# Head products of an attention kernel: from one 98-row product a head to pairs of heads on the array's row halves

## What is computed

```
n1 = ln(x); q, k, v = n1 @ wq[m] + bq, n1 @ wk[m] + bk, n1 @ wv[m] + bv
attn = softmax(q @ k.T / 4)                      # 512 x 512 for each of 2 x 16 heads
x = x + sum_m probs[m] * ((attn @ v) @ wo[m] + bo[m])
x = x + sum over the top 2 of 8 experts of gate * (gelu(ln(x) @ fw1[e]) @ fw2[e])
```

## Time and profile before

| | |
|---|---|
| median of 3 runs | 1408.23 us (1405.15 to 1408.82) |
| the profiled execution's own time | 1407.98 us |
| its span | 1406.2 us |
| mean granted clock | 0.995 |
| busy | PE 98%, DVE 76%, ACT 65%, POOL 26% |

### The profile page before, as it was taken

How to read it: one execution, slowest core, us unless ns; L and a number is a source line. 1 busy time by engine, 2 the same in 40 slices (tenths; PEclk the granted TensorE clock), 3 DMA queues, 4 the chain that set the end, 5 groups by cost and what they waited for, 6 DMA issues and landing times. The chain is left out here.

```text
span 1406.2 us, 22227 instructions
## 1 busy us (share of the span) xinstructions
PE 1380.4 (98%) x7666; PEld 714.5 (51%) x7666; DVE 1074.6 (76%) x2299; ACT 911.4 (65%) x1708; POOL 361.0 (26%) x351
## 2 busy tenths in 40 slices
PE   8999999999999999999999999999999999999989
PEld 6644445554455544456445654555445555354456
DVE  6789878977698777986879777897779868688631
ACT  3367567756667667776577666775676765657751
POOL 7422341302313223113322034132132222221000
PEclk9999999999999999999999999999999999999999
DMA  4065075321744136530662308441174415352002
GB/s 118 17 79 89 2 79 88 67 55 31 105 62 78 59 44 105 86 55 31 85 96 54 69 16 106 76 76 61 28 109 77 75 31 62 46 69 54 21 12 90
DMA packets 92307, 90.15 MB, mean 64 GB/s; under 512 B 16482, under 2 KB 87266, under 8 KB 91294
## 3 DMA queue, kind: packets, MB, share of 16 engines
q1 hardware_dynamic: 92196, 88.73, 38.1%
HBM read 35.05 MB, written 4.25 MB: 28 GB/s over the span
## 5 line engine op out<-in xcount | busy, mean ns | idle before, releaser
L1710 ACT ACTIVATE prob<-psum 128x512 f32<-128x512 f32 x1024 | 560.6, 600 | 317.9 <-PE psum L910 217.2
L1411 DVE TENSOR_REDUCE mx<-psum 128x1 f32<-128x512 f32 x1024 | 640.6, 681 | 77.8 <-PE psum L880 75.3
L895 PE MATMUL psum<-qst,kst 98*128 98x512 bf16 x1024 | 340.7, 382 | 2.3 <-DMA qst<-mrow 1.3
L880 PE MATMUL psum<-kst,qst 96*128 96x512 bf16 x1024 | 305.1, 381 | 5.5 <-DVE resid L1283 2.2
L910 PE MATMUL psum<-prob,vst 128*17 128x512 f32 x2048 | 246.6, 598 | 0.4 <-ACT prob L1710 0.2
L895 PEld LDWEIGHTS psum<-qst,kst 98*128 98x128 bf16 x1024 | 94.9, 98 | 202.8 <-issue 136.5
L880 PEld LDWEIGHTS psum<-kst,qst 96*128 96x128 bf16 x1024 | 97.5, 97 | 127.7 <-ACT prob L1710 17.1
L1861 POOL CAST parts<-resid 128x512 bf16<-128x512 f32 x64 | 39.4, 616 | 404.0 <-DVE resid L1283 404.0
L910 PEld LDWEIGHTS psum<-prob,vst 128*17 128x17 f32 x2048 | 46.7, 96 | 128.8 <-issue 109.8
L867 PE MATMUL psum<-w,cxT 128*128 128x256 f32 x448 | 105.1, 381 | 0.0
L848 PE MATMUL psum<-n2T,x 128*128 128x512 f32 x224 | 102.0, 592 | 0.0
(11 more groups left out here) (244 smaller groups left out, 1708.3 us busy)
## 6 DMA issues: line engine op xcount, KB each, us to landing
kst<-parts SPq DMA_DIRECT2D x186, 128.0 KB, 4.6
qst<-parts SPq DMA_DIRECT2D x186, 128.0 KB, 5.5
cmat<-G_dram SPq DMA_DIRECT2D x7, 1024.0 KB, 4.7
x<-in_L_ffn_fw SPq DMA_DIRECT2D x14, 512.0 KB, 3.6
w<-in_L_ffn_fw SPq DMA_DIRECT2D x14, 512.0 KB, 4.1
xbuf<-in_x SPq DMA_DIRECT2D x8, 512.0 KB, 5.2
kin<-in_ctx SPq DMA_DIRECT2D x8, 512.0 KB, 4.5
out<-acc SPq DMA_DIRECT2D x7, 512.0 KB, 3.9
```

The costliest lines, as they stand in the source:

```text
L880: e.matmul(psum[:, u.bank, :], qst[0:KROWS, h, t * P:(t + 1) * P], kst[0:KROWS, h, :], start=True, stop=True).then_inc(u.full, 1)
L895: e.matmul(psum[:, u.bank, :], kst[0:KROWS + 2, h, g * P:(g + 1) * P], qst[0:KROWS + 2, h, :], start=True, stop=True).then_inc(u.full, 1)
L1411: e.tensor_reduce(mx[:, qq * QUAD + j, t:t + 1], psum[:, u.bank, :], AX, ALU.max).then_inc(u.free, 1)
L1710: e.activation(prob[:, g % 2, j, :], psum[:, u.bank, :], ACT.Exp).then_inc(u.free, 1)
```

## The change

1. `kst` and `qst` become [128, 2, 16, 512]: partition halves for the two heads of a pair, a second index for the pass, 16 pairs. Pass 0 has the first four terms (64 rows a head); pass 1 has the last two terms, the two rows of the maximum, and zeros elsewhere.
2. A maximum is pass 0 alone: two products of 64 rows, on the row halves, into two neighbouring banks (`take_two`), and one reduction of 128 x 2 x 512. The last two terms are thus left out of the maximum, not of the score.
3. A score is two passes of two products, and one exponential of 128 x 1024.
4. The 32 maxima values of a quad are copied twice into `mxx`, transposed to 32 rows, and turned into both bf16 parts with a per-row factor `low` (0 or 1); one DMA sends them.
5. In the head: `kst[:, 1]` and `qst[:, 1]` are filled with zeros, the ones come from a bias `lift` or a DMA, the picks are 128 columns wide (32 instead of 48), and the weights are folded in half-size steps.
6. `AHEAD` counts pairs (64 in a batch), a score pair stands in each even slot, `VALUES` is 0 and all plans are new.

```diff
+            def take_two(*name):
+                both = banks.take_two(name, freed_at(clock[0], *name))
+                for u in both:
+                    if u.was is not None:
+                        e.wait_ge(u.was.free, u.was.n)
+                return both[0]
...
-                u = take("max", b, qq, j, t)
-                e.matmul(psum[:, u.bank, :], qst[0:KROWS, h, t * P:(t + 1) * P], kst[0:KROWS, h, :], start=True,
-                         stop=True).then_inc(u.full, 1)
+                u = take_two("max", b, qq, j, t)
+                for par in range(2):
+                    own = slice(HALF * par, HALF * (par + 1))
+                    ins = e.matmul(psum[:, u.both, :][:, par, :], qst[own, 0, h // 2, t * P:(t + 1) * P],
+                                   kst[own, 0, h // 2, :], start=True, stop=True)
+                ins.then_inc(u.full, 1)
...
-                u = take("score", b, qq, g, j)
-                e.matmul(psum[:, u.bank, :], kst[0:KROWS + 2, h, g * P:(g + 1) * P], qst[0:KROWS + 2, h, :], start=True,
-                         stop=True).then_inc(u.full, 1)
+                u = take_two("score", b, qq, g, j)
+                for i in range(2):
+                    for par in range(2):
+                        own = slice(HALF * par, HALF * (par + 1))
+                        ins = e.matmul(psum[:, u.both, :][:, par, :], kst[own, i, h // 2, g * P:(g + 1) * P],
+                                       qst[own, i, h // 2, :], start=i == 0, stop=i == 1)
+                ins.then_inc(u.full, 1)
...
-                e.tensor_reduce(mx[:, qq * QUAD + j, t:t + 1], psum[:, u.bank, :], AX, ALU.max).then_inc(u.free, 1)
+                e.tensor_reduce(mx[:, qq, :, j, t], psum[:, u.both, :], AX, ALU.max).then_inc(u.free, 1)
+                if j == PAIRS - 1 and t == NT - 1:
+                    e.wait_ge(u.free, u.n)
+                    src = mx[:, qq].rearrange("p r h t -> p r (h t)")
+                    e.tensor_copy(mxx[:], src.unsqueeze(2).to_broadcast([P, 2, 2, UNITS])).then_inc(maxima_in, 1)
...
-                e.tensor_scalar(mrow[:, q_ % 2, 0, :], src, -1.0, None, ALU.mult).then_inc(row_high, 1)
+                e.tensor_copy(mrow[:, q_ % 2, :], src).then_inc(row_high, 1)
...
-            e.memset(kst[KROWS:KROWS + 2, 0:HC, :], 1.0).then_inc(ones, 1)
+            e.memset(mrow[:], 1.0).then_inc(ones, 1)
+            e.memset(kst[:, 1], 0.0).then_inc(ones, 1)
...
-                e.activation(prob[:, g % 2, j, :], psum[:, u.bank, :], ACT.Exp).then_inc(u.free, 1)
+                e.activation(prob[:, g % 2, 2 * j:2 * (j + 1), :], psum[:, u.both, :], ACT.Exp).then_inc(u.free, 1)
...
+            e.memset(qst[:, 1], 0.0)
             e.memset(chosen, 0.0).then_inc(choice_made, 1)
...
-                for r in range(2):
-                    e.dma_start(qst[KROWS + r:KROWS + r + 1, qq * QUAD:(qq + 1) * QUAD, :], mrow[:, q_ % 2, r, :]
-                                ).then_inc(rows_in[q_ % 2], 16)
+                e.dma_start(qst[ROWS, 1, qq * PAIRS:(qq + 1) * PAIRS, :], mrow[:, q_ % 2, :]).then_inc(rows_in[q_ % 2], 16)
...
-        VALUES, COPY, TURN = 1, 3, 7
+        VALUES, COPY, TURN = 0, 3, 7
...
-            PE_S=slots(4, "p4:2 p5:15 p6 p7:14 v0:8 v1"),
+            PE_S=slots(5, "p4 p5:17 p6:0 p7:16 v0:14 v1"),
...
-            AHEAD="1300200300314230044012000010100221221000031300001011000104403001"
-                  "0020100321400001210130341010440001130110030202100012010003000000")
+            AHEAD="1000101110202110001110201010000011010010210000001000020202021000"
+                  "0000100202011021100100201020210000010002100100001010010010000000")
```

The middle batches' new tables for PE (A and C), beside those that they replace:

```diff
-            PE_A=slots(5, "kT0:4 kT1 qT0:0 qT1 gates:2 gsum:16 cols:17 cd0:0 cd1:5 st0:0 st1:0 st2:2 num0:8 num1:0 "
-                          "num2:2 num3:23 n1T0:0 n1T1 p0:5 p1 p2:7 p3:2 pv0:25 pv1:0 logits"),
-            PE_C=slots(-1, "cxT00:0 cxT01:13 cxT10:0 cxT11:2 wo0 wo1:0 wo2:5 wo3:17 mean:5 n2T0:3 n2T1:7 logits:6 hid00 "
-                           "hid01:0 hid02:2 hid03:2 eo00:2 eo01:2 eo02:0 eo03:7 hid10 hid11:0 hid12:0 hid13 eo10:3 "
-                           "eo11:5 eo12:11 eo13"),
+            PE_A=slots(5, "kT0:2 kT1:2 qT0:0 qT1:2 gates:2 gsum:15 cols:18 cd0:0 cd1:4 st0:0 st1 st2:3 num0:7 num1:2 "
+                          "num2:0 num3:21 n1T0:0 n1T1:2 p0:4 p1:3 p2:7 p3:2 pv0:25 pv1:0 logits"),
+            PE_C=slots(-1, "cxT00:0 cxT01:13 cxT10:0 cxT11:2 wo0:0 wo1:4 wo2:2 wo3:5 mean:20 n2T0:2 n2T1:6 logits:5 "
+                           "hid00:0 hid01 hid02 hid03:2 eo00:6 eo01:2 eo02:0 eo03:4 hid10:0 hid11:0 hid12:0 hid13:3 "
+                           "eo10 eo11:7 eo12:7 eo13"),
```

More of the change, by code:

```diff
@@ L57, in until, with hold @@
         return self.latest[k].until if self.latest[k] is not None else -1000
+    def hold(self, k, n, until, at=None):
+        at = k if at is None else at
+        self.taken += 1
+        self.order[k] = self.taken
+        self.latest[k] = Use(k, n, self.full[at], self.free[at], self.latest[k], until)
+        return self.latest[k]
     def take(self, name, until):
@@ L63, in take, with take_two @@
         self.counts[k] += 1
[L64 to L68, removed]
+        self.uses[name] = self.hold(k, self.counts[k], until)
+        return self.uses[name]
+    def take_two(self, name, until):
+        assert name not in self.uses
+        k = min(range(self.count - 1), key=lambda k: (max(self.until(k), self.until(k + 1)),
+                                                      max(self.order[k], self.order[k + 1])))
+        self.counts[k] += 1
+        one = self.uses[name] = self.hold(k, self.counts[k], until)
+        one.both = slice(k, k + 2)
+        return one, self.hold(k + 1, one.n, until, k)
 class Steps:
@@ L639, in stage_a @@
                         pick_first()
-                        for h in range(QUAD, HC):
+                        for h in range(PAIRS, HP):
                             yield f"pick{h}"
-                            for which in range(2):
-                                pick(which, [h])
+                            pick([(which, j, h) for which in range(2) for j in range(3)])
                     yield f"p{n}"
@@ L877, in maximum @@
                     for which in range(2):
-                        e.wait_ge(uses["pick", which, h].free, uses["pick", which, h].n)
-                u = take("max", b, qq, j, t)
-                e.matmul(psum[:, u.bank, :], qst[0:KROWS, h, t * P:(t + 1) * P], kst[0:KROWS, h, :], start=True,
-                         stop=True).then_inc(u.full, 1)
+                        for i in range(2):
+                            w = uses["pick", which, h // 2, i]
+                            e.wait_ge(w.free, w.n)
@@ L898, in values @@
+                ins.then_inc(u.full, 1)
             def values(b, qq, g):
                 q_ = b * NQ + qq
-                w = uses["score", b, qq, g, QUAD - 1]
+                w = uses["score", b, qq, g, PAIRS - 1]
                 e.wait_ge(w.free, w.n)
@@ L1173, in stage_a @@
                     residue(b, n)
-                if b == 0:
-                    u = uses["pick", 1, 0]
+                for i in range(0 if b else 2):
+                    u = uses["pick", 1, 0, i]
                     e.wait_ge(u.full, u.n)
-                    e.tensor_copy(qst[0:KROWS, 0, :], psum[0:KROWS, u.bank, :]).then_inc(u.free, 1)
+                    e.tensor_copy(qst[:, i, 0, :], psum[:, u.bank, :]).then_inc(u.free, 1)
                 yield "mean"
@@ L2119, in sync_program @@
             a.upto(-9)
[L2120 to L2122 removed]
+            e.wait_ge(ones, 2)
+            e.dma_start(kst[ROWS, 1, HP:, :], mrow[0:4, 0:1, :].to_broadcast([4, (M * H // 2 - HP) * S // P, P])).then_inc(ones_in, 16)
             until_maxima(a, first)
```

276 lines of the change are left out of this document (144 added, 132 removed), and 12 rows, old and new, of the table DVE_A.

## The result

The changed kernel takes 1428.86 us (median of 4 runs, 1425.87 to 1431.99), the kernel before 1406.69 beside it (4 runs, 1404.06 to 1408.82). The ratio is 1.0153, with a 95% interval of 1.013 to 1.0176: slower by 1.5%, where I had forecast 1.6% faster. The profiled execution took 1425.87 (span 1424.2, granted clock 0.995), 3.0 us under its median; before it was 1407.98 and 1406.2.

A forecast was written before the change was run, and what follows sets the result against it. PE's full queue was taken as the bound (busy 98% of the span); -110.6 + 50.6 + 27.1 + 6 + 3.9 = -23.0 us gave 1385 us, range 1352 to 1430.

The forecast's parts named there:

- The products: PE's maxima and scores: half-row products run beside each other, 0.22 us a pass, 512 maximum passes replacing 1024 products, -110.6 us.
- Rival C: Half-array bf16 weight loads cost as much as f32 ones: 1423 if at entries, near 1549 if every pass; chance 0.21.
- Changes of shape: PE's switches between array shapes: 516 more of them at 0.098 us each, +50.6 us.
- Second loads: Behind a change of shape PE's second weight load is not hidden, mainly for f32 products: +27.1 us.
- Rival B: Second weight loads are hidden behind 512-column products after all: -27, so 1358 us; chance 0.16.
- VectorE and ScalarE: Neither engine is the bound, but three pairs of banks leave less room than seven banks: PE waits +6 us.
- Rival D: Pairs of banks make PE wait, 0.2 us more at each of 128 value calls: +25, so 1410 us; chance 0.13.
- The head: Longer fills on VectorE and GpSimd delay the chain statistics, root, normalisation by 4.7 us; with small savings, +3.9 us.
- The sum: All terms for the whole kernel together: -23.0 us, so 1385 us.

The follow-up runs named there:

- e1: Kernel before, with only the maximum products cut to 64 of their 96 rows, number and order of instructions kept: 1503.77 us, ratio 1.067.
- e9: Changed kernel, with VectorE's maximum of a pair reading half of the columns: 1411.40 us, ratio 1.0032.
- e11: Changed kernel, with both VectorE's maximum and ScalarE's exponential on half of the columns: 1382.95 us, ratio 0.983.
- e6: Kernel before, own products and single banks, but two heads' products issued in succession at the changed kernel's table slots: 1441.26 us, ratio 1.0254.
- e5: Changed kernel, with GpSimd's fill of the query operand's second half cut in two and moved from in front of the first root: 1422.98 us, ratio 1.0118.
- e4: Changed kernel, with each pass one whole-array product of 128 rows instead of two of 64; VectorE and ScalarE read that bank twice: 1388.66 us, ratio 0.9848.
- e2: Kernel before, own whole-array products, but with the changed kernel's pairs of banks, instructions for two heads and tables of slots: 1455.08 us, ratio 1.0319.

## Why the prediction was wrong, step by step

- **The products.** Forecast -110.6, measured -111.8. The choice of 0.22 for a pass was right; half-row records start some 5 ns apart and the pass takes 0.22. Rival C is refuted: a second pass on the same half starts 0.21 behind the first, and the first behind a change costs about 0.011 more, as for whole-array bf16. (The rule of the Trainium skill, "TensorE: Matmul & The Clock Gate", section "The mechanism", that a load hides only behind another row group, is thus not borne out in this kernel.) That the measured time lies near C's 1423 is a coincidence of sizes.
- **Changes of shape.** +50.6 against +51.2. The account holds the count (516 forecast, 522 measured; the forecast's own tables add to 515) at a fixed price; the price is confirmed by the median distances, 0.097 here and 0.099 in e1, which has 888 more and a span 93.5 us longer with their second loads.
- **Second loads.** +27.1 against +23.5. Rival B is refuted by the 1.98 us runs and by e1's +17.5.
- **VectorE and ScalarE: the step that failed.** It said "I take +6 us, between 0 and +30". Waiting measured outside the first 100 us: 60.3 instead of 19.0, +41.3, beyond my upper end. What it got right is the cause it named, room: 0.66 us of PE against 1.14 us of VectorE. Four things in it were wrong. At the value calls it weighed the products' wait for the exponential, which the first group covers, and not the exponential's wait for the products: at the call at 616.67 its banks then come back at 2.20 instead of 1.78 us. It priced the waits at those calls alone; they are spread over maxima, scores and transposes. It took comfort in averages (VectorE near 76% of the span), but an average says nothing of the bursts in which PE meets three long instructions in a row, as near 715 us. And it looked at each engine by itself, whereas e9 to e11 show that PE is held by whichever of two is late, so that relief of one is worth little. It never asked what issuing heads by twos costs with unchanged instructions; in the kernel before, e6 has that at 36 us, in tables that were not made for it. Rival D was this mechanism, with a price of +25 and a chance of 0.13; both were too low.
- **The head.** +3.9 against 10.1 at the first score, and 13.7 of waiting in the first 100 us. The part worked out, GpSimd's fill in front of the root, came as told (free at 12.66, root 4.6 late), and e5 gets 5 us back. VectorE's own fill took 3.47 and not 6.9, but since the root waited for GpSimd that did not matter. What I subtracted (shorter picks, one DMA less) did not come: the picks start 5.9 later (65.84 against 59.97), and from there to the first score it is 4.2 more, with a wait of 3.2 for the copy of the maxima in it (before it was 1.7), and 1.7 us lost to the half clock behind that wait, which no term of the forecast had.
- **The sum.** -1.2 in the stream, +0.6, -3.6, +35.3 in the waits and +9.8 in the head: +41 on -23 gives the +18. The time lies in the range, at its dear end, by luck: the range reached that far for the dearer weight loads of rival C, which did not come.

How much of the waiting is due to twos, to banks in pairs and to shorter products is not told apart in the changed kernel itself. Nor is whether more banks would remove the waits, or only shorter instructions: the maxima and scores have seven banks and the value sums the eighth. No version here that does the whole computation beats the kernel before. The head's fix leaves 1423; with both engines halved, which no full computation allows, it would be 1383. Before any wait, 75 us more of changes and second loads stand against the 112 saved.

## What to carry to other kernels

When PE's queue gets shorter, price the return: put the other engines' time for one unit beside PE's time for it, count the units that fit between, and give the waits a term of their own size (here 41 us outside the head against the 112 saved in the stream; in e4 some 30 of 73 did not come through). Handling two tiles as one halves the instruction count but also doubles the grain in which buffers come back; try the grain alone, with the work unchanged (as e2 and e6 do), before building on it. And when one engine's relief gains little, relieve two before you rule out the mechanism.

## What the runs showed of the hardware

- GpSimd's fill held short VectorE instructions of the same time: started at 8.36, five of them ended together at 12.69, GpSimd's fills at 12.66; with the fill gone each of the five lasts 0.16 or 0.17. VectorE's own fill (3.47) and its statistics (1.40) ran beside the same fill and lasted as long as before. The Trainium skill, "SBUF — State Buffer", section "SBUF: two separate sides", has an exclusive lock on a port pair that VectorE, in some modes, and GpSimd share, held for the whole instruction; the trace agrees, with 4.2 us of holding, over the end of one fill and the whole of the next.
- VectorE fills 128 x 8192 bf16 as 4096 32-bit words in 3.47 us, GpSimd the same number of bf16 in 6.98.
- A transfer of 128 KB into 32 partitions, every fourth one, lands in 2.1 us where the one into 16 neighbouring partitions took 4.6 and 5.5 (keys and queries), and the mean busy share of the DMA engines fell from 38% to 19% at the same bytes. I had not looked at it; the profile's issue list after:

```profile
kst<-parts SPq DMA_DIRECT2D x186, 128.0 KB, 2.1
```
